# Attention reordered on one core: centre taps on ScalarE, weighted values turned round, masks added on TensorE

## The reference

```python
x = x + L0_conv(_gn(x))       # channel attention, 8 heads of 12 channels
x = L1_conv(x)                # pointwise and 13x13 depthwise convolution, gelu
t = _to_tokens(x)             # 16 x 256 tokens x 96
t = t + L2_attn(_ln_t(t)); t = t + L2_ffn(_ln_t(t))    # L2: the diagonal is masked
t = t + L3_attn(_ln_t(t)); t = t + L3_ffn(_ln_t(t))    # L3: causal
# L0: qkv = depthwise 3x3 (nine taps) of x @ w_qkv; q and k scaled to norm one; softmax over 12x12 per head
# L2, L3: qkv = x @ w; scores = q k^T * scale, 6 heads of 16
scores = jnp.where(masked, -jnp.inf, scores)
weights = jax.nn.softmax(scores, axis=-1)
out = weights @ v             # per head
out = out @ w_proj + b_proj
```

## Time and profile before

| | |
|---|---|
| median of 3 runs | 1038.35 us (1035.98 to 1043.4) |
| the profiled execution | 1034.51 us, span of the trace 1032.5 us |
| mean granted clock of TensorE | 0.937 of 2.4 GHz |
| busy: PE, PEld | 886.7 us (86%), 791.0 us |
| busy: DVE, ACT, POOL | 598.4 us (58%), 424.0 us (41%), 318.0 us (31%) |

### The profile page before, as it was taken

The page is one execution under the profiler, slowest core; times in us unless marked ns, Lnnn a source line. Parts: engine busy times, 40 slices in busy tenths (PEclk is TensorE's granted clock), DMA queues, the critical chain, the costliest instruction groups (busy, mean ns, idle before and its releaser), DMA issues. The chain is left out here.

```text
span 1032.5 us, 19657 instructions
## 1 busy us (share of the span) xinstructions
PE 886.7 (86%) x6482; PEld 791.0 (77%) x6482; DVE 598.4 (58%) x1824; ACT 424.0 (41%) x667; POOL 318.0 (31%) x375
## 2 busy tenths in 40 slices
PE   2988868995499999996999998489899969999997
PEld 1766657884388888995999997278888858888887
DVE  5999974536467666643556554257667633444443
ACT  0355542003134444334555554133444335545653
POOL 3111118602022334114333432222333142343332
PEclk9999988997599999997999999569999988999999
DMA  3730000000633333300000000334433200000000
GB/s 78 163 50 0 0 1 1 0 0 1 132 70 75 69 69 69 69 1 1 1 0 0 0 0 1 81 76 92 98 69 80 58 1 1 10 14 8 8 8 16
DMA packets 27560, 37.87 MB, mean 37 GB/s; under 512 B 9288, under 2 KB 24352, under 8 KB 27424
## 3 DMA queue, kind: packets, MB, share of 16 engines
q1 hardware_dynamic: 27520, 37.36, 17.1%
HBM read 25.06 MB, written 12.29 MB: 36 GB/s over the span
## 5 line engine op out<-in xcount | busy, mean ns | idle before, releaser
L1429 PE MATMUL ps<-w,ff_b_h 128*128 128x96 f32 x1536 | 181.8, 275 | 6.7 <-ACT ff_b_fT L1485 6.7
L1429 PEld LDWEIGHTS ps<-w,ff_b_h 128*128 128x128 f32 x1536 | 178.5, 192 | 10.5 <-issue 7.3
L1496 ACT ACTIVATE ff_b_h<-ps,b 128x512 f32<-128x512 f32 x192 | 128.7, 687 | 121.6 <-PE ps L1421 121.4
L1032 PE MATMUL ps<-values,at_b_pT 128*128 128x102 f32 x1344 | 162.0, 277 | 1.2 <-POOL at_b_pT L957 0.9
L1032 PEld LDWEIGHTS ps<-values,at_b_pT 128*128 128x128 f32 x1344 | 155.6, 193 | 3.6 <-issue 1.6
L1569 DVE SCALAR_TENSOR_TENSOR tok<-ps,ff_b_gate,tok 128x96 f32 (+1 forms) x224 | 56.0, 311 | 136.0 <-PE ps L1429 136.0
L957 POOL TENSOR_SCALAR_AFFINE_SELECT at_b_pT<-at_b_pT 128x768 f32<-128x768 f32 x64 | 54.6, 865 | 240.9 <-ACT at_b_pT L1142 240.3
L1205 DVE TENSOR_REDUCE at_b_mf<-ps 128x6 f32<-128x1536 f32 (+1 forms) x64 | 98.1, 1552 | 26.5 <-PE ps L1009 25.9
L1142 ACT ACTIVATE at_b_pT<-ps 128x1536 f32<-128x1536 f32 x64 | 80.9, 1291 | 43.3 <-PE ps L1017 43.1
L611 DVE SCALAR_TENSOR_TENSOR ca_qk<-ps,dw,ca_qk 96x225 f32<-96x225 f32 (+1 forms) x256 | 98.7, 447 | 0.0
L1007 PE MATMUL ps<-keys,at_b_qs 96*128 96x256 bf16 (+1 forms) x384 | 71.3, 274 | 23.8 <-issue 21.0
(11 more groups left out here) (227 smaller groups left out, 1486.5 us busy)
## 6 DMA issues: line engine op xcount, KB each, us to landing
at_parts<-at_b_part SPq DMA_DIRECT2D x96, 96.0 KB
at_b_qs<-at_parts SPq DMA_DIRECT2D x16, 288.0 KB, 4.2
keys<-at_parts SPq DMA_DIRECT2D x16, 288.0 KB, 5.2
at_b_qs<-at_parts SPq DMA_DIRECT2D x16, 192.0 KB, 5.7
keys<-at_parts SPq DMA_DIRECT2D x16, 192.0 KB, 6.3
w<-in_L_ffn_w SPq DMA_DIRECT2D x4, 576.0 KB
chan<-in_x SPq DMA_DIRECT2D x4, 384.0 KB, 5.4
at_b_qs<-at_parts SPq DMA_DIRECT2D x16, 96.0 KB, 6.4
```

Of the source, the lines that this page charges most:

```text
L1032: ins = nc.tensor.matmul(ps[:, 6 + u, OW * t:OW * (t + 1)], pT[:, u, k, h, P * t:P * (t + 1)], vp[:, slot, u, k, h, :], start=(n == 0), st ...
L1429: ins = nc.tensor.matmul(ps[:, 6 + e % 2, C * t:C * (t + 1)], h[:, e % 2, j, P * t:P * (t + 1)], f.w2[:, e * HC + j, :], start=(j == 0), s ...
L1496: nc.scalar.activation(h[:, e % 2, j, :], ps[:, 3 * (e % 2) + j, :], ACT.Gelu, bias=f.b1[:, e * HC + j:e * HC + j + 1]).then_inc(s_h, 1)
```

## The change

- Channel attention: the centre taps of q and k are made by ScalarE (`centre_tap`, two activations with a scale per channel), in its list between `keep_turned` and `keep_product`; VectorE keeps eight taps each and its step waits for `s_centre`.
- Token attention: PSUM is three areas of two banks, and scores, maxima, transposed scores and exponentials go in units of four heads' blocks (1024 columns; in layer 3 four and two blocks of 256 and six of 128): three units per image where there were two.
- `transposed_scores` adds the mask by a product of its own to each block; `masked` on GpSimd is gone.
- `weighted_values` is turned round: v (128 x 32 per head: 16 values, one column of ones, zeros) is stationary, the exponentials stream. The outputs of four heads lie on partitions 0, 32, 64 and 96. ScalarE copies the result (`keep_weighted`), TensorE turns it (`turn_weighted`, three fp32 transposes), then `out` as before.
- q and k of both images are split in one go (`high`, `rests`, `middle`, `lows`). The copies of `xT` and of v and both `rows` copies are on ScalarE. The maxima have two bf16 parts in place of three.
- The lists of all engines are written anew as one `body` per pair, in which the first image's exponentials belong to the pair itself and the second's to the pair before. SyncE loads the stacks of a pair only after all transposed scores of the pair two before (`s_ST`).

The diff, cut and less indented; for the token attention the new text alone, since the old one stands above:

```diff
-VD = D + 1
-MAX_ROWS = 3 * H
-OW = H * VD
+VW = 2 * D
+MAX_ROWS = 2 * H
...
+    def centre_tap(b, slot):
+        act.wait_ge(s_qk, b + 1)
+        for t in range(2):
+            nc.scalar.activation(qkc[:, slot, t, :], ps[0:C, slot, N * t:N * (t + 1)], ACT.Copy,
+                                 scale=m.dw0[:, t, 4:5]).then_inc(s_centre, 1)
...
             keep_turned(b - 1)
+        if ahead:
+            centre_tap(b + 1, other)
         if back == 2:
...
-                if n == 0:
-                    nc.vector.tensor_scalar(dst, src, m.dw0[:, t, k:k + 1], None, ALU.mult).then_inc(s_tap[t], 1)
-                    continue
-                dve.wait_ge(s_tap[t], 9 * b + n)
+                if n > 1:
+                    dve.wait_ge(s_tap[t], 8 * b + n - 1)
...
-        dve.wait_ge(s_qk, b + 1)
-        if back:
-            dve.wait_ge(s_T, b)
-        convolve(b, slot, 0, 2)
+        dve.wait_ge(s_centre, 2 * b + 2)
+        convolve(b, slot, 1, 2)
...
+    if causal:
+        score_units = [[(1, h, N * h, N) for h in range(4)], [(1, h, N * (h - 4), N) for h in (4, 5)],
+                       [(0, h, P * h, P) for h in range(H)]]
+        weight_units = [[(0, h, N * h, N) for h in range(4)], [(0, h, N * (h - 4), N) for h in (4, 5)],
+                        [(1, h, P * h, P) for h in range(H)]]
+    else:
+        score_units = [[(b // H, b % H, N * (b % 4), N) for b in range(4 * k, 4 * k + 4)] for k in range(3)]
+        weight_units = score_units
...
+    def area(r):
+        return ps[:, 2 * r:2 * r + 2, :].rearrange("p k n -> p (k n)")
+    def unit(r, blocks):
+        width = blocks[0][3]
+        return area(r)[:, 0:width * len(blocks)].rearrange("p (b n) -> p b n", n=width)
...
+    S_AREA = ((0, 1, 0), (1, 2, 1))
+    T_AREA = ((0, 2, 0), (2, 1, 2))
+    QK_AREA, V_AREA = 0, 1
...
         sp.wait_ge(s_part, 96 * i + 96)
+        if back:
+            sp.wait_ge(s_ST, 6 * i - 6)
...
-    def masked(i, u):
-        for t in range(TPI):
-            block = pT[:, u, t, :, P * t:P * (t + 1)]
-            pool.wait_ge(s_ex, 4 * i + 2 * u + t + 1)
-            alone(pool, m)
-            pool.affine_select(out=block, in_=block, compare_op=ALU.is_ge if causal else ALU.not_equal, fill=0.0,
-                               base=0, pattern=[[0, H], [1, P]], channel_multiplier=-1).then_inc(s_zero, 1)
...
+    def transposed_scores(i, slot, u, k):
+        for t, h, at, width in weight_units[k]:
+            out = area(T_AREA[u][k])[:, at:at + width]
+            nc.tensor.matmul(out, ks[:, slot, h, u, P * t:P * (t + 1)], qs[:, slot, h, u, N - width:N],
+                             start=True, stop=False)
+            own = P * t - (N - width)
+            ins = nc.tensor.matmul(out[:, own:own + P], mask[:, :], m.ident_b[:, :], start=False, stop=True)
         ins.then_inc(s_ST, 1)
...
+    def weighted_values(i, slot, u):
+        for k in range(TPI):
+            pe.wait_ge(s_ex, 6 * i + 3 * u + k + 2)
+            n0 = P if causal and k else 0
+            for h in range(4):
+                nc.tensor.matmul(ps[32 * h:32 * (h + 1), 6 + u, n0:N], vp[:, slot, u, k, h, :], pT[:, u, k, h, n0:N],
+                                 start=(k == 0), stop=(k == TPI - 1), skip_group_check=True)
+        for k in range(TPI):
+            for t in range(k if causal else 0, TPI):
+                for h in (4, 5):
+                    g = 2 * t + h - 4
+                    ins = nc.tensor.matmul(ps[32 * g:32 * (g + 1), 6 + u, N:N + P], vp[:, slot, u, k, h, :],
+                                           pT[:, u, k, h, P * t:P * (t + 1)], start=(k == 0),
+                                           stop=(k == (t if causal else TPI - 1)))
+        ins.then_inc(s_W, 1)
+    def turn_weighted(i, u):
+        pe.wait_ge(s_os, 2 * i + u + 1)
+        for t in range(TPI):
+            nc.tensor.transpose(ps[:, 6 + u, 192 * t:192 * t + P], oS[:, u, t, :], m.ident[:, :])
+        ends = ps[:, 6 + u, 0:2 * 192].rearrange("p (t c) -> p t c", t=2)[:, :, P:192]
+        nc.tensor.transpose(ends, oS[:, u, 2, :], m.ident[:, :]).then_inc(s_O, 1)
...
@@ TensorE @@
+    def body(i, slot, back, ahead, nxt):
         pe.wait_ge(s_stack[slot], 48 * (i - slot) + 96)
+        if back:
+            pe.wait_ge(s_ex, 6 * i - 3)
+        else:
+            pe.wait_ge(s_r1, i + 2)
         scores(i, slot, 0, 0)
+        pe.wait_ge(s_vp, i + 1)
+        scores(i, slot, 0, 1)
+        if back == 2:
+            turn_out(i - 2, 1)
+        if back:
+            pe.wait_ge(s_mr, 2 * i)
+            pe.wait_ge(s_ex, 6 * i - 4)
+            transposed_scores(i - 1, 1 - slot, 1, 0)
+        pe.wait_ge(s_mx, 6 * i + 1)
+        scores(i, slot, 0, 2)
+        if back:
+            weighted_values(i - 1, 1 - slot, 0)
+        if back == 2:
+            project(i - 2, 1)
+        if back:
+            pe.wait_ge(s_mx, 6 * i + 2)
+            transposed_scores(i - 1, 1 - slot, 1, 1)
+            turn_weighted(i - 1, 0)
+        if back == 2:
+            pe.wait_ge(s_tk, 2 * i - 1)
+        if ahead:
+            turn(i + 2)
+        if back:
+            pe.wait_ge(s_ex, 6 * i - 2)
+            transposed_scores(i - 1, 1 - slot, 1, 2)
+        if ahead:
+            pe.wait_ge(s_xT, i + 3)
+        turn_maxima(i, 0)
+        if ahead:
+            pe.wait_ge(s_mx, 6 * i + 3)
+            queries_keys(i + 2, slot)
+        if back:
+            pe.wait_ge(s_ex, 6 * i - 1)
+        else:
+            pe.wait_ge(s_mx, 6 * i + 2)
+        scores(i, slot, 1, 0)
+        if back:
+            pe.wait_ge(s_ex, 6 * i)
+        scores(i, slot, 1, 1)
+        pe.wait_ge(s_mr, 2 * i + 1)
         if back:
             turn_out(i - 1, 0)
+            weighted_values(i - 1, 1 - slot, 1)
+        if ahead:
+            pe.wait_ge(s_r1, i + 3)
+        else:
+            pe.wait_ge(s_mx, 6 * i + 3)
+        transposed_scores(i, slot, 0, 0)
+        pe.wait_ge(s_mx, 6 * i + 4)
+        scores(i, slot, 1, 2)
         if back:
             project(i - 1, 0)
+        pe.wait_ge(s_mx, 6 * i + 5)
+        transposed_scores(i, slot, 0, 1)
+        if back:
+            turn_weighted(i - 1, 1)
+        pe.wait_ge(s_ex, 6 * i + 1)
+        transposed_scores(i, slot, 0, 2)
+        if nxt:
+            pe.wait_ge(s_mx, 6 * i + 6)
+            values(i + 1, 1 - slot)
+        if back:
+            pe.wait_ge(s_tk, 2 * i)
         turn_maxima(i, 1)
...
@@ ScalarE @@
+    def values(i, slot):
+        act.wait_ge(s_v, i + 1)
+        nc.scalar.copy(vp[:, slot, :, :, :, 0:D].rearrange("p u t h d -> p (u t h) d"),
+                       area(V_AREA)[:, 0:4 * C].rearrange("p (k d) -> p k d", d=D)).then_inc(s_vp, 1)
+    def weights(i, u, k):
+        blocks = weight_units[k]
+        act.wait_ge(s_ST, 6 * i + 3 * u + k + 1)
+        n0 = TPI * N - N - blocks[0][3]
+        dst = pT[:, u, :, :, :].rearrange("p t h n -> p (t h) n")
+        b0 = H * blocks[0][0] + blocks[0][1]
+        nc.scalar.activation(dst[:, b0:b0 + len(blocks), n0:N], unit(T_AREA[u][k], blocks), ACT.Exp).then_inc(s_ex, 1)
+    def rows(i, slot, u):
+        act.wait_ge(s_M, 2 * i + u + 1)
+        nc.scalar.copy(qs[C:KR, slot, :, u, :], max_rows(u)).then_inc(s_mr, 1)
+    def keep_weighted(i, u):
+        act.wait_ge(s_W, 2 * i + u + 1)
+        nc.scalar.copy(oS[:, u, :, :].rearrange("p t n -> p (t n)"), ps[:, 6 + u, 0:3 * P]).then_inc(s_os, 1)
...
+    def body(i, slot, back, ahead, nxt):
+        if back == 2:
+            out(i - 2, 1)
+        if back:
+            weights(i - 1, 1, 0)
+            keep_weighted(i - 1, 0)
+            weights(i - 1, 1, 1)
+        if ahead:
+            normed(i + 2, slot)
+        if back:
+            weights(i - 1, 1, 2)
+        rows(i, slot, 0)
+        if ahead:
+            high(i + 2)
+        if back:
+            out(i - 1, 0)
+            keep_weighted(i - 1, 1)
+        weights(i, 0, 0)
+        if ahead:
+            middle(i + 2)
+        weights(i, 0, 1)
+        weights(i, 0, 2)
+        if nxt:
+            values(i + 1, 1 - slot)
+        rows(i, slot, 1)
...
@@ VectorE @@
+    def rests(i):
+        dve.wait_ge(s_p1, i + 1)
+        nc.vector.tensor_tensor(rest[:, :, :, :].rearrange("c t u n -> c (t u n)"), area(QK_AREA)[0:C, :],
+                                part[:, 0, :, :, :].rearrange("c t u n -> c (t u n)"), ALU.subtract).then_inc(s_r1, 1)
...
+    def maximum(i, u, k):
+        blocks = score_units[k]
+        dve.wait_ge(s_S, 6 * i + 3 * u + k + 1)
+        b0 = H * blocks[0][0] + blocks[0][1]
+        nc.vector.tensor_reduce(mf[:, u, :, :].rearrange("p t h -> p (t h)")[:, b0:b0 + len(blocks)],
+                                unit(S_AREA[u][k], blocks), AX.X, ALU.max, negate=True).then_inc(s_mx, 1)
...
+    def body(i, slot, back, ahead, nxt):
         maximum(i, 0, 0)
         maximum(i, 0, 1)
+        maximum(i, 0, 2)
         maxima_parts(i, 0)
+        if back == 2:
+            add(i - 2, 1)
+        if back:
+            out(i - 1, 0)
```

(50 more changed lines are left out.)

331 lines of the change are left out of this document (117 added, 214 removed).

## The result

| | before | after |
|---|---|---|
| median | 1039.09 us (1035.98 to 1043.4, 4 runs) | 968.88 us (965.6 to 970.21, 4 runs) |
| ratio | | 0.932, 95% interval 0.928 to 0.936 |
| profiled execution, span | 1034.51, 1032.5 us | 970.21, 968.5 us |
| mean granted clock | 0.937 | 0.921 |

The account below looks back on a forecast made before the run. VectorE was taken to bound channel attention and TensorE both token attentions; -9 - 25 - 22 + 4 = -52 us against the profiled 1034.5, plus 3.8 for the median of the runs, gave 986 us, range 943 to 1035.

Parts of the forecast that it names:

- What bounds the kernel: VectorE bounds channel attention (49.5 of 50 us busy); TensorE bounds both token attentions (48.8 and 46.1).
- half rate: Token attention: weighted-values products overlap only partly across quarters, taking 5.2 and 3.9 us a pair, half of 10.4 and 7.8.
- rival A: Token attention: products in four quarters run at once, 2.6 and 1.95 us a pair, total 951 us; chance 0.2.
- column price of 1.69 ns: TensorE, token attention: cost of one streamed fp32 column, giving 10.4 and 7.8 us a pair without overlap.
- Masks and turn_weighted: TensorE, token attention: 24 mask products add 1.5 us a pair, six fp32 transposes add 0.65 us.
- finer pieces: First token attention: 0.3 us of added waits a pair, because work is handed over in smaller units.
- The ring that was weighed: Channel attention: ScalarE's loop with centre taps takes 6.6 to 7.2 us; turn taken as 6.9, gain 9 us.
- Rival D: Channel attention: the change has no effect, ring at 7.4, 9 us less gain, inside the range; no separate chance given.
- the sign named in the forecast: Channel attention: VectorE idle before its first tap, waiting on the centre taps, would show the forecast wrong.
- The starts: Start of each token attention: parts handed over whole, not by halves, with nothing covering it, +2 us twice.
- rival B: Token attention: new waits, chiefly ScalarE's rows copy before transposed scores, eat half the gain, 1010 us; chance 0.17.
- SyncE's new wait: Token attention: stack loads wait for transposed scores two pairs back; done at 15.7 us, covered with 4 us to spare.

Follow-up runs that it names:

- experiment 3: Changed kernel without the mask products on the transposed scores, leaving the masking of the weights out: 958.34 us, ratio 0.924 to the kernel before.
- experiment 1: Changed kernel with every weighted-values product sent to the first quarter, and division by the sums replaced by multiplication by a constant: 1068.35 us, ratio 1.029.
- experiment 9: Changed kernel with mask products on transposed scores removed and GpSimd clearing the masked weights instead: 963.93 us, ratio 0.928.
- Experiments 7: Changed kernel with only each attention's last pair reordered on ScalarE and TensorE, weighted values ahead of the previous pair's projection: 965.03 us, ratio 0.930.
- 11: Changed kernel with GpSimd masks and three order edits, but TensorE masks for the second half of each attention's last pair: 946.56 us, ratio 0.9125.

## Why the forecast came out as it did

- **What bounds the kernel.** Right for the token attentions: TensorE leads before and after, and leaving 1.44 us of its work out shortens the turn (experiment 3), though only by half of it.
- **Weighted values (the failed step).** The forecast had "the second must follow the first, and only the second of one head runs beside the first of the next", hence half rate, 5.2 and 3.9 us. Measured were 2.9 and 2.4: rival A's rate, 0.11 us for 256 columns. The column price of 1.69 ns was right (3.48/2048 = 1.70 in experiment 1). What failed was to turn the order of issue into a limit on what runs at once. It is 8 x 2.3 + 8 x 1.5 = 30 us of gain left out of the forecast. The Trainium skill (TensorE: Matmul & The Clock Gate, Packing small matmuls) has 2.38 times for three column groups; this case shows 3.95 for four, close to one for each group. Both speak against the half rate. The drain of which the Trainium skill (TensorEngine Tiling, Key Properties) tells costs 0.1 us at most here: the first product starts 0.15 us behind the last mask (330.86, 331.01), where the next block would have started after 0.06.
- **Masks and turn_weighted.** Right: a transposed block with its mask takes 0.17 us, without 0.11, and the three transposes of an image 0.33. Not seen was that half of what leaving them out saves is lost at once to ScalarE's round (experiment 3), and that GpSimd could have kept them (experiment 9).
- **Turns.** 20.4 and 18.2 forecast, 17.74 and 16.89 measured. With 2.9 and 2.4 for the weighted values the forecast's sum gives 23.56 - 10.8 + 2.9 + 1.5 + 0.65 = 17.8 in the first, and 20.94 - 8.1 + 2.4 + 1.5 + 0.65 - 0.7 = 16.7 in the second. The 0.3 that the forecast allowed for finer pieces in the first is left out here; with it the sum is 18.1. So all but that one term held within 0.4 us.
- **Channel attention.** The ring that was weighed went by ScalarE alone. The real one goes bounded squares, GpSimd, scaled keys, turn, result and value taps on TensorE, scores, maximum, and back to bounded squares through two taps: 7.28 us, from 82.99 to the same instruction at 90.27. VectorE's lost work turned into its wait of 0.48. Rival D, "the ring at 7.4", is what happened. (The forecast's 7.49 - 6.9 is 0.59, not 0.55; 9 us stands either way.) At the start the second image's taps waited 2.64 us for ScalarE's centre taps, the sign named in the forecast as one of being wrong.
- **The starts.** They cost +0.6 and +0.8, not +2 each.
- **The ends**, priced at nothing, cost 14 us. Two things are seen in the traces. The new order puts more of the next pair ahead of the first weighted values (TensorE begins 125 instructions between the first scores and them, before 81 and 80), and they come 5.6 and 6.3 us later. And before, the last pair had a long run of weighted values with nothing to wait for, 72 instructions (36 products) in 8.3 us; these products are short now. That this run covered the last round trips is read from the order and was not tested by itself. The low clock has a smaller share. By an estimate from the windows view in steps of 1 us (busy time of TensorE times the part of the clock not granted), it cost 4.6 and 6.3 us in the two attentions before and 7.2 and 8.4 after, so 2.6 and 2.1 of the 14. Experiments 7 and 11 show part of the last pair's cost as curable; no experiment changed the first bodies.
- **New waits (rival B).** Present, and small: the products wait 4.9 + 3.1 us in all for rows copies, 0.6 to 0.9 a pair in the second attention. **ScalarE** at 13.4 us a pair (37.80/50 x 17.74) was forecast at 13.5. **VectorE** was put at 14 to 15 and is at 12.4 (34.86/50 x 17.74), which costs nothing, since it isn't the bound; reductions of 1024 columns, forecast at 1.22, took 1.217. **SyncE's new wait** is covered in the steady turn; keys come late for the last pair of each attention only, by 0.4 and 1.1 us.
- **The sum.** Span: -52 forecast; -32 for the turns (30 of them the weighted values), +8 for channel attention, +14 for the ends, -3 for the starts, rounding 1: -64, which is what was measured. So 986 came within 2% partly by luck: a gain left out (30 us) and two costs left out (8 and 14 us) stood against each other.

## What to carry to other kernels

Small products whose outputs lie in different quarters of the partitions ran side by side here, in both orders that were tried. Where operands can be turned so that they do, a quarter of the column price is what this case measured for four quarters. Then look at what the long run of products had been covering: the ends of the stage, and the one ring through all engines that the relieved engine is part of. Where an operation is cheap on the bound engine and slow on an idle one, the steady turn and the end of a stage may want it in different places, for at the end nothing is hidden.

## What the runs showed of the hardware that was not expected

Four streams of fp32 products, two instructions each, ran 3.95 times as fast in four quarters as in one, also with four instructions of one quarter in a row (0.88 us both ways). The same waits of 2.17 and 2.18 us were followed by the low clock in one run and by the full clock in another; behind it, the same products took 2.55 us or 1.44.
